# A perceiver layer on one core: context loads moved behind a group's last crossbar transfer, and the mixing block's numerator and denominator moved to GpSimd

## What is computed

```python
x = x + xattn(layernorm(x), ctx_768, Wq, Wk, Wv, Wo, bo)     # 16 heads of 64, softmax over 257 rows
x = x + attn(layernorm(x), mix_k, mix_v, mix_r, ...)          # the mixing block
x = x + ffn(layernorm(x), Wr, br, W1, b1, W2, b2)             # 8 experts, one per token (argmax)
```

```python
k = (x * mix_k + x_prev * (1 - mix_k)) @ W_key.T        # v and r alike; r through a sigmoid
exp_k = exp(k); exp_ek_v = exp_k * v
state_a, state_b = ...                                  # decayed exclusive prefix sums over time
num = state_a + exp_u * exp_k * v
den = maximum(state_b + exp_u * exp_k.sum(-1, keepdims=True), 1e-06)
return r * (num / den) @ W_output.T
```

## Time and profile before

| | |
|---|---|
| median of three runs | 1282.58 us |
| profiled execution, its own time | 1273.21 us |
| its span (first to last instruction) | 1271.0 us |
| TensorE, VectorE, ScalarE, GpSimd busy | 72%, 63%, 55%, 36% of the span |
| mean granted TensorE clock | 0.844 of full |
| DMA engines of the hardware queue, busy | 40.5% |

### The profile page before, as it was taken

The page is one execution under the profiler, slowest core; times in us unless marked ns, Lnnn a source line. Parts: engine busy times, 40 slices in busy tenths (PEclk is TensorE's granted clock), DMA queues, the critical chain, the costliest instruction groups (busy, mean ns, idle before and its releaser), DMA issues.

```text
span 1271.0 us, 26427 instructions
## 1 busy us (share of the span) xinstructions
PE 911.3 (72%) x7018; PEld 696.0 (55%) x7018; DVE 799.9 (63%) x2759; ACT 702.5 (55%) x2157; POOL 451.8 (36%) x981
## 2 busy tenths in 40 slices
PE   7667786767686877777777777677768873504996
PEld 6455565555565655556565656565556652504664
DVE  5677766666666665757575757575757776522564
ACT  4655665655565565656565656565646641303774
POOL 4333423232323232333333323232333333074554
PEclk9898888888888887888887878887888895556998
DMA  8544444444444444444443434343434429011120
GB/s 206 92 92 93 92 92 93 92 92 92 92 91 91 91 91 91 91 91 91 91 91 80 103 75 103 79 94 83 96 79 104 79 56 217 18 51 45 52 55 23
DMA packets 323072, 112.16 MB, mean 88 GB/s; under 512 B 274606, under 2 KB 320817, under 8 KB 323008
## 3 DMA queue, kind: packets, MB, share of 16 engines
q1 hardware_dynamic: 320704, 107.14, 40.5%
q0 software_dynamic: 2304, 4.25, 1.1%
HBM read 37.25 MB, written 7.52 MB: 35 GB/s over the span
## 4 chain that ended last, share of the span: by engine, by line
PE 49%; DMA 14%; DVE 13%; issue 8%; POOL 6%; ACT 6%; SPq 2%; POOLq 0%; DVEq 0%; ACTq 0%
PE bank L389 14%; PE quad L367 13%; DMA PT<-PHL 13%; PE bank L378 4%; PE bank L407 4%; DVE PHL L760 3%; PE quad L1320 3%; ACT quad L663 3%; PE bank L395 2%; POOL sorted_rows L1186 2%; PE bank L1335 2%; DVE rec L842 2%; DVE nmax L729 1%; POOL xm L934 1%; ACT PHL L669 1%
## 5 line engine op out<-in xcount | busy, mean ns | idle before, releaser
L389 PE MATMUL bank<-PT,chi 128*96 128x512 f16 x512 | 192.1, 464 | 178.9 <-DMA PT<-PHL 166.5
L669 ACT ACTIVATE PHL<-quad,rsum 128x256 f16<-128x256 f32 x512 | 201.6, 487 | 199.6 <-DMA PT<-PHL 169.6
L663 ACT ACTIVATE quad<-quad,nmax 128x257 f32<-128x257 f32 x512 | 228.7, 447 | 118.1 <-DVE nmax L729 117.4
L367 PE MATMUL quad<-rawT,qf 96*128 96x257 f32 x1024 | 259.4, 398 | 3.0 <-DVE PHL L760 2.3
L729 DVE TENSOR_REDUCE nmax<-quad 128x1 f32<-128x257 f32 x512 | 199.0, 419 | 64.6 <-PE quad L367 61.6
L760 DVE SCALAR_TENSOR_TENSOR PHL<-quad,rsum,PHL 128x256 f16<-128x256 f32 x512 | 219.7, 476 | 0.0
L367 PEld LDWEIGHTS quad<-rawT,qf 96*128 96x128 f32 x1024 | 201.3, 203 | 32.5 <-issue 2.9
L389 PEld LDWEIGHTS bank<-PT,chi 128*96 128x96 f16 x512 | 64.3, 146 | 222.9 <-issue 192.0
L758 DVE TENSOR_TENSOR p<-quad,rsum 128x2 f32<-128x2 f32 x256 | 39.6, 155 | 198.6 <-ACT PHL L669 196.3
L677 ACT ACTIVATE Oh<-bank 96x512 f16<-96x512 f32 x128 | 76.1, 595 | 91.3 <-PE bank L395 89.2
L663 ACT ACTIVATION_READ_ACCUMULATOR quad<-quad,nmax 128x1 f32 x512 | 103.3, 202 | 0.0
(11 more groups left out here) (219 smaller groups left out, 2006.6 us busy)
## 6 DMA issues: line engine op xcount, KB each, us to landing
rawT<-in_dram SPq DMA_DIRECT2D x32, 385.5 KB, 3.9
raw<-in_dram SPq DMA_DIRECT2D x32, 384.0 KB, 4.4
sorted_rows<-fill SPq DMA_DIRECT2D x1, 2620.0 KB, 23.4
xs<-sorted_rows SPq DMA_DIRECT2D x40, 65.5 KB, 1.8
R<-in_dram SPq DMA_DIRECT2D x4, 512.0 KB, 5.2
Z<-last_rows SPq DMA_DIRECT2D x128, 2.2 KB
PT<-PHL SPq DMA_TRANSPOSE x128, 4.5
w1r<-in_dram SPq DMA_DIRECT2D x4, 512.0 KB, 14.3
```

The costliest lines, as they stand in the source:

```text
L367: nc.tensor.matmul(bank[t][:, 0:M], qf[:, gpar, b, t * P:(t + 1) * P], rawT[:, gpar, b, :], start=True, stop=True).then_inc(s_S, 1)
L389: nc.tensor.matmul(bank[5][0:CC, :], w[:, s8, c, :], p, start=(k == 0), stop=False)
L663: nc.scalar.activation(bank[t][:, 0:M], bank[t][:, 0:M], ACT.Exp, bias=nmax[:, p, t:t + 1], accum_out=sums[:, p, t:t + 1]).then_inc(s_exp, 1)
L669: nc.scalar.activation(PHL[:, p, t, 0, :], bank[t][:, 0:MK], ACT.Identity, scale=rsum[:, p, t:t + 1])\
```

## The change

It does three things. The context load moves from behind the crossbar transfer of a group's first batch (jj = 0) to behind that of its last (jj = 3), and the `Z` load from jj = 1 to jj = 2. GpSimd makes `chi` and `clo` three batches ahead, not four, so it asks for the raw context of a group one step later. And `den` and `num`, each one multiply-and-add on VectorE, become a product and a sum each on GpSimd, in step -1 behind `dx`, through a new tile `prod`; `denm` stays on VectorE.

```diff
+        prod = sb("prod", [P, MT])
...
-            if j == -1 and chunk(it, 3) is not None:
-                c = it - 3
-                wait(nc.vector, s_m["dm"], c)
-                wait(nc.vector, s_m["esum"], c + 1)
-                wait(nc.vector, s_m["sst"], 2 * c + 1)
-                nc.vector.scalar_tensor_tensor(den[:, :], esum[:, :], nlw[:, 1:2], sst[:, 1, :], ALU.mult, ALU.add)\
-                    .then_inc(s_m["dn"], 1)
...
-                wait(nc.vector, s_m["o"], c)
-                wait(nc.vector, s_m["sst"], 2 * c + 2)
-                nc.vector.scalar_tensor_tensor(num[:, :], ekv[:, :], nlw[:, 1:2], sst[:, 0, :], ALU.mult, ALU.add)\
-                    .then_inc(s_m["num"], 1)
...
-            if exists(n + 4):
-                if (j + 4) % GB == 0:
-                    wait(nc.gpsimd, s_ctx[((j + 4) // GB) % NP2], 16 * (it + 1 + ((j + 4) // GB - ((j + 4) // GB) % NP2) // NP2))
-                pool_prep(n + 4, (j + 4) % NC8, ((j + 4) // GB) % NP2, (j + 4) % GB)
+            if exists(n + 3):
+                if (j + 3) % GB == 0:
+                    wait(nc.gpsimd, s_ctx[((j + 3) // GB) % NP2], 16 * (it + 1 + ((j + 3) // GB - ((j + 3) // GB) % NP2) // NP2))
+                pool_prep(n + 3, (j + 3) % NC8, ((j + 3) // GB) % NP2, (j + 3) % GB)
...
+            if j == -1 and chunk(it, 3) is not None:
+                c = it - 3
+                wait(nc.gpsimd, s_m["dm"], c)
+                wait(nc.gpsimd, s_m["esum"], c + 1)
+                wait(nc.gpsimd, s_m["o"], c)
+                fb = nlw[:, 1:2].broadcast_to([P, MT])
+                nc.gpsimd.tensor_tensor(prod[:, :], esum[:, :], fb, ALU.mult).then_inc(s_m["prod"], 1)
+                wait(nc.gpsimd, s_m["sst"], 2 * c + 1)
+                wait(nc.gpsimd, s_m["prod"], 2 * c + 1)
+                nc.gpsimd.tensor_tensor(den[:, :], prod[:, :], sst[:, 1, :], ALU.add).then_inc(s_m["dn"], 1)
+                wait(nc.gpsimd, s_m["dn"], c + 1)
+                nc.gpsimd.tensor_tensor(prod[:, :], ekv[:, :], fb, ALU.mult).then_inc(s_m["prod"], 1)
+                wait(nc.gpsimd, s_m["sst"], 2 * c + 2)
+                wait(nc.gpsimd, s_m["prod"], 2 * c + 2)
+                nc.gpsimd.tensor_tensor(num[:, :], prod[:, :], sst[:, 0, :], ALU.add).then_inc(s_m["num"], 1)
...
-                if jj == 0 and exists(g + 2, G) and (n_static(n) is None or g >= 0):
+                if jj == 3 and exists(g + 2, G) and (n_static(n) is None or g >= 0):
                     load_ctx(g + 2, gp)
-                if jj == 1 and exists(g + 1, G) and (n_static(n) is None or g >= 1):
+                if jj == 2 and exists(g + 1, G) and (n_static(n) is None or g >= 1):
                     load_z(g + 1, 1 - gp)
...
-            for b in range(GB - 1):
+            for b in range(GB - 2):
                 pool_prep(b, b, 0, b)
```

More of the change, by code:

```diff
@@ L217, in perceiver_layer_kernel @@
                                           "esum", "dx", "mdx", "xm", "ekv", "fab", "cs", "st", "scl", "sst", "dn", "num", "dm",
-                                          "rec", "o", "y", "res", "stat3")}
+                                          "rec", "o", "y", "prod", "res", "stat3")}
         s_w3 = sem("s_w3")
```

## The result

The changed kernel takes **1090.07 us** (median of 4 runs, 1088.17 to 1093.84) against 1281.23 of the kernel before in the runs beside it: ratio 0.8513, 95% interval 0.848 to 0.8545. That is 191 us less, where 165 were forecast; the range of 1085 to 1160 holds it. The profiled execution took 1089.03 us.

The account below looks back on a forecast made before the run. It took the kernel to be bound by crossbar transfers issued late, once per group, behind SP's wait for scores. Minus 203 plus 38 us gave minus 165: 1273.2 to 1108 profiled, plus 9.4 hence 1117 us, range 1085 to 1160.

Parts of the forecast that it names:

- The sum of 203 us: Stalls removed by moving the context load: 6.9 us in step 6 and 6.6 in step 2, 15 of each.
- step 2: One of the two long steps of an eight-batch iteration holding a late transfer: from 13.21 us to 6.6.
- Transfers beside the load: Crossbar transfers issued near the moved context load still arrive in time: nothing lost, at most 33 us in all.
- Rival A: The load makes transfers miss their room of 8.1 us by 1 to 3 us per group: 1150 to 1205; chance 0.14.
- D: Slower than before: the queue holds transfer 4g+4 until transfer 4g+3 and both loads land: about 1325 us; chance 0.02.
- E: SP's wait stays behind transfer 4g+3 and only the GpSimd cost is new: about 1320 us; chance 0.02.
- den and num on GpSimd: In step -1, `denm` waits for `den` behind `dx`: 2.4 us more, 16 times, 38 us in all.
- rival C: VectorE's `denm` and GpSimd's product for `num` exclude each other, 0.4 to 0.7 us in 16 places: 1123 to 1128; inside forecast's 0.70.
- the late `e12p`: GpSimd makes the next batch's `e12p` only after `num`, at about 536.0 to 536.5; ScalarE's exponentials cover it: nothing.
- Step 0: Step after -1: slow TensorE products at 1.2 GHz make step 1's `nmax` 1.3 late, absorbed there: nothing, upper bound 18 us.
- step 1: Third long step, where TensorE waits 3.64 us for GpSimd's `e12p`: left alone at 9.67 us, about 8.0 if the clock is back.
- rival B: Less stall in the mixing block: steps 0 and 1 run short, by early arrival or high clock: 1075 to 1093; chance 0.12.

Follow-up runs that it names:

- the kernel without this stand: The changed kernel, but GpSimd's product for `num` waits for VectorE's `denm`: 1090.38 us, ratio 0.8503 to the kernel before.

## Why the prediction was right, and where its sizes were off

**The mechanism** was right: SP's wait for the group's last scores held transfer 4g+1, once per group. Its size was met by two errors that cancel. The sum of 203 us was read from one trace, and the two profiled executions, before and with the loads alone moved, are 202.7 us apart (1273.21 and 1070.52). But an iteration from 3 to 14 lost 14.3 us and not 13.5, and the first three, whose stalls were shorter, 11.0 each; that the two made up for each other is luck. The larger loss per iteration comes from the stall's aftermath in step 2. There I took off VectorE's idle time of 6.64 us and nothing else, but VectorE also stood for the `v` product of TensorE before it could make `ekv`:

```profile
561.62 0.42 DVE L857 TENSOR_TENSOR ekv<-ek,bank 128x256 f32<-128x256 f32 x1 [1.58 <-PE bank L650]
```

Step 2 came out at 5.44 us, not 6.6. The medians are 215 us apart. The further 12 us lie between executions and not between the traces: the profiled execution of the kernel before took 8.6 us less than the median of the runs beside the loads-only kernel, and that kernel's own profiled execution 3.9 more than its median. No kept trace shows where.

**Transfers beside the load**: nothing lost, as taken. Rival A is out, and the run with the load at jj 1 shows roughly how far the room goes. D and E fell with it.

**den and num on GpSimd**: right in sign and mechanism; off in both parts of its size. Step -1 grew by 3.05 us, not 2.4. Of the difference 0.44 is `denm` standing for the shared port (rival C, true for `denm`; the product kept its 0.61, and the kernel without this stand is no faster). The other 0.2 are the late `e12p`, which I had put at nothing: by it `dx` starts 6.25 us after the step began and not 5.86, and half of that comes back since `dx` no longer takes 0.83. Step 0 grew by 0.8 from the low clock; I had named 1.3 as the bound and taken nothing, holding that step 1 would absorb it.

**The term that was wrong** is step 1, "The change leaves it alone": 9.67 forecast, 7.18 measured. The working had it as a bound only ("if the clock is back in step 1, that step falls from 9.67 to about 8.0"), and gave it to rival B, whose first half is what happened. The stand in step -1 moves the low clock into step 0. In the profiled executions that leaves 0.8 us for each of the 13 iterations from 3 to 15, together 11 us in place of 31. The two iterations of the drain are not spared: from the last step's start to the end the kernel takes 256.0 us and with the loads alone 248.2, 3.9 us each where 2.4 were forecast. Together that is the 18.5 us between these two executions; by the medians 23 of the 38 us remained.

Together: 165 us less forecast, 203 off and 38 on; 191 less measured by the medians, 215 off by the loads and about 23 on by the rest. Between the profiled executions it is 184 less, 203 off and 18.5 on: there the forecast missed by 19 us, and all of that is the second part.

## What to carry to other kernels

A load's place in an issuing queue is to be chosen by its waits, not by its transfer time: it belongs where everything that it waits for has been waited for anyway. Whoever moves an operation to another engine should ask which instruction stands directly ahead of it there and what that one waits for; the same four operations cost 19 us behind `dx` and nothing that could be measured ahead of it. And a stand of TensorE can cost its aftermath at the low clock too (here behind stands of 2.9 to 3.9 us), and can move or fill the next stand. The same operations cost 17 to 26 us where step 1 had a long stand of its own and 50 where it had none, so a stall is to be priced with its neighbours.

## What the hardware showed that was not expected

- One stall can pay for part of the next: with a stand of 3.12 us ahead of step 0, steps 0 and 1 have clocks of 0.77 and 1.00 and take 14.5 us together; without it 1.00 and 0.69 and, in the iteration shown, 17.5 (16.9 in the mean of 13).
- Twelve products of no use in such a stand make a kernel of 1067 us 26 to 30 us faster, though the wait that they stand in is as long as before.
- GpSimd's `dx` takes 0.61 us alone, 0.83 beside one VectorE operation with two SBUF inputs (`denm`), and 1.14 in the kernel with `e12p` first, where it begins between `num` and `denm`; `denm` takes 0.42 alone and 0.86 behind a GpSimd product that began 0.04 us earlier.
